# Attention over 64 row tiles: where V's bias, the output copy and one exponential stand in a tile, and x's normalisation as a three-operand pass

## The chip, the cores and the metric

The program runs on one core of a Trainium2 chip. The metric is the device time of one execution in microseconds (us); the kernel before takes 6042.36 us (median of 3 runs, 6042.21 to 6044.77). The engines are named as in the profile: PE (TensorE matmul), PEld (its weight load), DVE (VectorE), ACT (ScalarE), POOL (GpSimd), SP (SyncE, which issues the DMAs here).

## The reference, cut to what matters

Four layers run one after the other over x of shape (8, 1024, 256), each on a layer-normalised input and with a residual. Only the first is touched:

```
x = x + attn(layernorm(x))            # 16 heads of 16, per batch of 1024 rows
  q, k, v = x@Wq.T+bq, x@Wk.T+bk, x@Wv.T+bv
  logits  = li[:, :, None, :] + lj[:, None, :, :] + rel_b      # 3 relations for each pair (i, j)
  bias    = einsum('bijk,hk->bhij', softmax(logits), logical_bias)
  gate    = sigmoid(x @ gate_W.T + gate_b)                     # one for each row and head
  scores  = q.k/sqrt(16) + gate*bias
  out     = softmax(scores) @ v @ Wo.T + bo
x = x + fp8 layer;  x = x + mixer and MLP;  x = x + gated FFN  # unchanged
```

## The kernel before, in words

`attention` works through 64 tiles of 128 query rows, 8 tiles to a batch. A tile is a hand-written software pipeline: each engine has a `body` that loops `for u in range(H)` over the 16 heads, and the `if` lines in it say after which head the side work stands. Every engine runs its list strictly in that order; the engines meet at semaphores.

The main line for head h: PE makes the scores in `ps_s` (`pe_s`, L647); DVE adds the relation bias to the row (`dve_f`, L491, for 12 heads; POOL does it for heads 1, 4, 8 and 12 in two passes, L408 and L410); DVE adds the scores and takes the row minimum (`dve_s`, L502, a pass and a short read of the accumulator, called s(h) here); ACT takes the exponential (`act_e`, L576, e(h)); PE transposes the row (`pe_t`, L658, t(h)); ACT copies it to `AT` (`act_at`, L585, AT(h)); PE multiplies by V (`pe_pv`, L670). There is one `ps_s`, so PE's scores of head h+1 wait for s(h).

Side work, some for this tile, some for others:

- x's normalisation, one tile more than a batch ahead: `dve_ln` (u = 2), `pool_rstd`, then `dve_xn` (L440, u = 5), which frees the x buffer and lets PE transpose it (`pe_xT`, u = 6).
- V's bias: PE makes V and the gate's logits in `ps_m` at u = 3 (`pe_v`, L635); `dve_v` adds the biases (L455 to V, L459 to `zg`). `ps_m` is shared by many small products in a fixed order (`pm`, `pm_free`).
- The output of the tile before: ACT copies `ps_o` out (`act_o`, L589), PE transposes it (`pe_oT`, L680, u = 5; it also needs `dve_v` to have released `ps_m`), DVE normalises (`dve_norm`, L508 and L510, u = 6).
- The relation probabilities of the next tile: DVE L474 and L477, POOL L382 twice, ACT three exponentials, POOL sums them (L387, L391), ACT takes the logarithm and then the exponential of it, a reciprocal (`act_y0`, L568 and L571), POOL multiplies (L395), DVE corrects (`dve_y`, L482, u = 10), POOL multiplies twice (L400).

The first 56 tiles also prepare a tile of the next batch (`pro` is true); the last 8 don't, and have no `dve_xn` and no `dve_v`. `look` (there is a next tile) and `post` (there is one before) are true nearly always.

Of the kernel before, what the change touches and what calls it, by code (L numbers as in the profile page):

```python
# [13 lines left out]
P = 128  # L14
# [3 lines left out]
B, S, D = 8, 1024, 256  # L18
# [16 lines left out]
def wait(eng, sem, value):  # L35

    if isinstance(value, int) and value <= 0:
        return
    eng.wait_ge(sem, value)
# [10 lines left out]
def attention(nc, x_in, wqk, wvg, bqk, rows, ident_in, parts_d, x_out):  # L50
# [13 lines left out]
    with ExitStack() as ctx:  # L64
# [3 lines left out]
        def sem(name):  # L68
            HELD["done"].append(ctx.enter_context(nc.semaphore(name)))
            return HELD["done"][-1]  # L70
# [28 lines left out]
        xt = sb("xt", [P, 2, D])  # L99
        stats = sb("stats", [P, 6])  # L100
        mv = sb("mv", [P, 2])
        ve = sb("ve", [P, 1])
        mhalf = sb("mhalf", [P, 1])
        rstd = sb("rstd", [P, 1])
        xn = sb("xn", [P, D])
# [61 lines left out]
        x_free = sem("x_free")  # L167
# [269 lines left out]

        def dve_xn(dve, p, k):
            wait(dve, rstd_ok, p + 1)
            nc.vector.tensor_scalar(xn[:], xt[:, k, :], mv[:, 0:1], rstd[:, 0:1],  # L440
                                    ALU.subtract, ALU.mult).then_inc(x_free, 1)

        def dve_qk(dve, p):
            wait(dve, gT_ok, p + 1)
# [39 lines left out]
        def dve_f(dve, t, k, h):  # L484
            if h in POOL_HEADS:
                return
            r = rows_sb[h % NROW]
            if h == 0:
                wait(dve, pc_ok, t + 1)
            wait(dve, t_ok, 2 * (H * t + h) + 2)  # L490
            nc.vector.scalar_tensor_tensor(r[:], ps_p[:], rho[:, h:h + 1], R[k][0][:],  # L491
                                           ALU.mult, ALU.add).then_inc(fd_ok, 1)

        def dve_s(dve, t, k, slot, h):

            if h in POOL_HEADS:
                wait(dve, fp_ok, NPH * t + POOL_HEADS.index(h) + 1)
            else:
                wait(dve, fd_ok, NDH * t + DVE_HEADS.index(h) + 1)
            alone(dve, qk_ok, H * t + h + 1, dve_own)  # L500
            r = rows_sb[h % NROW]
            nc.vector.tensor_tensor_reduce(r[:], r[:], ps_s[:], small[:, slot, h:h + 1], BIG, ALU.add, ALU.min,  # L502
                                           nmax[:, h % NROW:h % NROW + 1]).then_inc(s_ok, 1)
# [50 lines left out]
        def act_rel(act, t, k, slot, step):  # L554
            if step == 0:
                wait(act, rel_step, 2 * t + 2)
                nc.scalar.activation(R[k][0][:], RT[:], ACT.Exp, scale=-1.0).then_inc(rel_exp, 1)
            else:
                wait(act, rel_d, 2 * t + step)
                dst = (R[k][1], R2)[step - 1]  # L560
                nc.scalar.activation(dst[:], dst[:], ACT.Exp,
                                     bias=small[:, slot, H + step - 1:H + step]).then_inc(rel_exp, 1)

        def act_y0(act, t, step):

            if step == 0:
                wait(act, rel_sum, 2 * t + 2)
                nc.scalar.activation(R2[:], RT[:], ACT.Ln).then_inc(rel_y0, 1)  # L568
            else:
                act.wait_ge(rel_y0, 2 * t + 1)  # L570
                nc.scalar.activation(R2[:], R2[:], ACT.Exp, scale=-1.0).then_inc(rel_y0, 1)  # L571

        def act_e(act, t, h):
            wait(act, s_ok, H * t + h + 1)
            r = rows_sb[h % NROW]
            nc.scalar.activation(r[:], r[:], ACT.Exp, scale=-1.0, bias=nmax[:, h % NROW:h % NROW + 1]  # L576
                                 ).then_inc(e_ok, 1)
# [9 lines left out]
        def act_o(act, o):  # L587
            wait(act, pv_ok, 2 + HG * (o + 1))
            nc.scalar.copy(O4[:], ps_o[:]).then_inc(o_ok, 1)  # L589
# [166 lines left out]
        def after(par, ib, n):  # L756

            return (par * NT + ib + n) % (2 * NT)

        def followed(t, pro):  # L760

            return t > 0 and t <= (B - 1) * NT if isinstance(t, int) else pro
# [137 lines left out]
        def _(dve):  # L900
# [51 lines left out]
            def body(dve, t, k, par, ib, pro, post, look, before):  # L952
                for u in range(H):
                    if u + 1 < H:
                        dve_f(dve, t, k, u + 1)
                    dve_s(dve, t, k, after(par, ib, 0), u)
                    if look and u < 2:
                        dve_rel(dve, t + 1, 1 - k, after(par, ib, 1), u)
                    if pro and u == 2:
                        dve_ln(dve, t + AHEAD, 1 - k)  # L960
                    if u == 3 and (not isinstance(t, int) or t >= 2):
                        dve_out(dve, t - 2)
                    if pro and u == 5:
                        dve_xn(dve, t + AHEAD, 1 - k)
                    if pro and u == 4:
                        dve_v(dve, t + NT, 1 - par, ib)
                    if post and u == 6:
                        dve_norm(dve, t - 1)
                    if look and u == 10:
                        dve_y(dve, t + 1)  # L970
                    if pro and u == 13:
                        dve_gate(dve, t + NT)
                    if pro and u == 14:
                        dve_qk(dve, t + AHEAD)
                    if look and u == 15:
                        dve_f(dve, t + 1, 1 - k, 0)
# [68 lines left out]
        @block.scalar  # L1045
        def _(act):
            def start(act):
                act.wait_ge(w_ready, 1)
                act_g_t(act, 0)
                act_xT(act, NT)  # L1050
                act_g_d(act, 0)
                act_g_e(act, 0)
                act_d(act, NT, NT)
                for s in range(2):
                    act_g_hi(act, 0, s)
                act_g_t(act, 1)
                for s in range(2):
                    act_g_mid(act, 0, s)
                act_g_ge(act, 0)
                act_g_d(act, 1)  # L1060
                act_g_e(act, 1)
                act_rel(act, 0, 0, 0, 0)
                act_rel(act, 0, 0, 0, 1)
                act_rel(act, 0, 0, 0, 2)
                for s in range(2):
                    act_g_hi(act, 1, s)
                for s in range(2):
                    act_g_mid(act, 1, s)
                for step in range(2):
                    act_y0(act, 0, step)  # L1070
                act_p(act, 0, 0)
                act_hi(act, NT)
                act_g_ge(act, 1)
                act_mid(act, NT)
                act.wait_ge(g_st, 16 * 8)

            def body(act, t, k, par, ib, pro, post, look, before):
                for u in range(H):
                    act_e(act, t, u)
                    if post and u == 5:  # L1080
                        act_o(act, t - 1)
                    if pro and u == 7:
                        act_xT(act, t + AHEAD)
                    if look and u in (7, 8):
                        act_y0(act, t + 1, u - 7)
                    if u >= LAG:
                        act_at(act, t, u - LAG)
                    elif post:
                        act_at(act, t - 1, H + u - LAG)
                    if u == 0 and (not isinstance(t, int) or t >= 2):  # L1090
                        act_aT(act, t - 2)
                    if followed(t, pro) and u == 0:
                        act_hi(act, t - 1 + AHEAD)
                    if followed(t, pro) and u == 2:
                        act_mid(act, t - 1 + AHEAD)
                    if look and u in (1, 3, 4):
                        act_rel(act, t + 1, 1 - k, after(par, ib, 1), (1, 3, 4).index(u))
                    if pro and u == 6:
                        act_gate(act, t + NT, 1 - par, ib)
                    if pro and u == 10:  # L1100
                        act_d(act, t + AHEAD, after(par, ib, AHEAD))
                    if look and u == 13:
                        act_p(act, t + 1, 1 - k)

            def finish(act):
                for u in range(H - LAG, H):
                    act_at(act, TILES - 1, u)
                act_aT(act, TILES - 2)
                act_o(act, TILES - 1)
                act_aT(act, TILES - 1)  # L1110

            act.preload_act_table_set("natural_log_exp_and_others")
            act.sem_inc(at_ok, 2)
            run(act, start, body, finish)
# [1298 lines left out]
```

## Time and profile before

| | us |
|---|---|
| median of 3 runs | 6042.36 (6042.21 to 6044.77) |
| the profiled execution | 6042.3 |
| its span | 6040.5 |
| attention in it | about 2870: `dve_norm` of the last tile stands at 2866.8 |
| one tile of the first 56, in step | 43.27 |
| one tile of the last 8 | 42.08 |

The page shows the profile of one execution. Inside attention the four compute engines are all busy over three quarters of the time, so the page's shares don't name the one that bounds it; the order of events in one tile does. After the first few tiles the tiles repeat to within some hundredths of a us, but for two or three, so one tile can be read for all.

### The profile page before, as it was taken

What the parts mean: (1) busy time and instruction counts of PE and PEld (TensorE: products, weight loads), DVE (VectorE), ACT (ScalarE), POOL (GpSimd) and SP (SyncE); (2) the same over time, 40 slices, a digit from 0 to 9 for tenths busy, and PEclk for the clock granted to TensorE, in tenths of its full rate; (3) what the DMA queues carried; (4) which work ended last, traced back from release to release, by engine and by line L of the source; (5) the groups of instructions that cost most, each with busy time, mean ns of one, the idle gap of its engine ahead of it and who ended that gap; (6) DMA issues with size and microseconds to landing.
All of it is one profiled execution on the core that took longest, in us unless ns stands there. A gap on an engine that the chain in (4) does not pass through costs nothing. (4 is left out here: it accounts for less than half of the span.)

```text
span 6040.5 us, 114022 instructions
## 1 busy us (share of the span) xinstructions
PE 5365.8 (89%) x40162; PEld 3532.6 (58%) x40162; DVE 4701.5 (78%) x6099; ACT 4409.7 (73%) x7005; POOL 3704.9 (61%) x2010
## 2 busy tenths in 40 slices
PE   6888888898989898888799869999999979999999
PEld 4666666666666666655344345555555546666665
DVE  6999999999999999998888679999999942122221
ACT  4999999999999999999366678888888821111111
POOL 3888888888888888875100079999999930000000
PEclk8999999999999999999899889999999989999999
DMA  2121121212112121200355555555555521111110
GB/s 74 28 49 31 28 51 28 51 28 51 28 34 45 30 48 31 46 17 14 129 190 211 187 211 187 208 208 191 195 201 207 184 101 42 45 35 35 35 35 11
DMA packets 461255, 537.80 MB, mean 89 GB/s; under 512 B 237537, under 2 KB 337761, under 8 KB 460785
## 3 DMA queue, kind: packets, MB, share of 16 engines
q1 hardware_dynamic: 460784, 531.75, 28.0%
q8 instruction: 268, 4.39, 0.3%
q14 instruction: 203, 1.66, 0.1%
HBM read 370.31 MB, written 161.35 MB: 88 GB/s over the span
## 5 line engine op out<-in xcount | busy, mean ns | idle before, releaser
L502 DVE CUSTOM_DVE_ANT_0 srow<-srow,ps_s,small 128x1024 f32<-128x1024 f32 x1024 | 1304.0, 1273 | 63.5 <-issue 34.6
L576 ACT ACTIVATE srow<-srow,nmax 128x1024 f32<-128x1024 f32 x1024 | 1200.0, 1172 | 87.3 <-DVE nmax L502 78.3
L585 ACT COPY AT<-ps_t 128x512 f32<-128x512 f32 x2048 | 1110.5, 604 | 19.8 <-PE ps_t L658 18.8
L658 PEld LDWEIGHTS ps_t<-ident,srow 128*128 128x128 f32 x8192 | 954.9, 141 | 224.2 <-issue 36.3
L658 PE MATMUL ps_t<-ident,srow 128*128 128x128 f32 x8192 | 1068.7, 273 | 2.8 <-ACT AT L585 2.4
L1977 POOL TENSOR_TENSOR c_hc<-c_hs,c_cs 128x1024 f32<-128x1024 f32 x432 | 1009.9, 2364 | 61.2 <-DVE c_hs L2079 59.1
L491 DVE SCALAR_TENSOR_TENSOR srow<-ps_p,rho,R 128x1024 f32<-128x1024 f32 x768 | 975.3, 1270 | 0.0
L1938 PE MATMUL c_ps_y<-c_hc,c_ident 128*128 128x512 f32 x2048 | 944.8, 594 | 29.9 <-DVE c_y L2062 21.4
L2079 DVE TENSOR_TENSOR_SCAN c_hs<-c_da,c_pd 128x1024 f32<-128x1024 f32 x384 | 860.1, 2273 | 54.6 <-PE c_pd L1929 54.6
L647 PE MATMUL ps_s<-K,Q 96*128 96x512 bf16 x2048 | 617.1, 383 | 291.2 <-DVE nmax L502 265.3
L2022 ACT ACTIVATE c_sT<-c_dxT,c_bT 128x256 f32<-128x256 f32 x1536 | 668.4, 494 | 107.0 <-PE c_pd L1929 96.9
L410 POOL TENSOR_TENSOR srow<-srow,R 128x1024 f32<-128x1024 f32 x256 | 608.1, 2375 | 46.9 <-POOL srow L408 46.9
L670 PE MATMUL ps_o<-AT,V 128*32 128x128 f32 x16384 | 607.4, 278 | 0.0
L2215 POOL TENSOR_TENSOR d_rstd<-d_ve,d_mhalf 128x4 f32<-128x4 f32 x16 | 16.3, 1017 | 899.1 <-DVE d_ve L1222 899.1
L1938 PEld LDWEIGHTS c_ps_y<-c_hc,c_ident 128*128 128x128 f32 x2048 | 359.5, 190 | 344.9 <-issue 314.0
L1929 PEld LDWEIGHTS c_pd<-c_ident,c_sT 128*128 128x128 f32 x3072 | 353.9, 142 | 340.0 <-issue 198.1
L1929 PE MATMUL c_pd<-c_ident,c_sT 128*128 128x128 f32 x3072 | 407.4, 276 | 106.8 <-DVE c_hc L2086 79.6
L670 PEld LDWEIGHTS ps_o<-AT,V 128*32 128x32 f32 x16384 | 401.3, 109 | 129.3 <-issue 128.5
L2013 ACT ACTIVATE c_da<-c_dt,c_a_neg 128x1024 f32<-128x1024 f32 x384 | 435.8, 1135 | 1.7 <-issue 1.7
L647 PEld LDWEIGHTS ps_s<-K,Q 96*128 96x128 bf16 x2048 | 144.4, 97 | 476.0 <-DVE nmax L502 342.9
L1970 POOL TENSOR_TENSOR c_db<-c_dx,c_bs 128x1024 f32<-128x1024 f32 x128 | 302.1, 2361 | 121.4 <-DMA c_bs<-bc_d 121.4
L2242 DVE TENSOR_TENSOR d_x<-d_ps_y,d_y 128x512 f32<-128x512 f32 x32 | 22.1, 691 | 438.6 <-PE d_ps_y L2317 438.6
(256 smaller groups left out, 8576.5 us busy)
## 6 DMA issues: line engine op xcount, KB each, us to landing
c_cs<-bc_d SPq DMA_DIRECT2D x256, 512.0 KB, 4.3
c_bs<-bc_d SPq DMA_DIRECT2D x64, 512.0 KB, 6.5
Q<-parts_d SPq DMA_DIRECT2D x384, 64.0 KB, 2.3
parts_d<-parts SPq DMA_DIRECT2D x57, 384.0 KB, 3.4
K<-parts_d SPq DMA_DIRECT2D x168, 128.0 KB, 4.4
sz_d<-b_sz SPq DMA_DIRECT2D x16, 1024.0 KB, 7.1
xv_d<-b_xv SPq DMA_DIRECT2D x16, 1024.0 KB, 7.8
dt_d<-b_ab SPq DMA_DIRECT2D x16, 1024.0 KB, 4.2
```

Of the source, the lines that this page charges most:

```text
L491: nc.vector.scalar_tensor_tensor(r[:], ps_p[:], rho[:, h:h + 1], R[k][0][:], ALU.mult, ALU.add).then_inc(fd_ok, 1)
L502: nc.vector.tensor_tensor_reduce(r[:], r[:], ps_s[:], small[:, slot, h:h + 1], BIG, ALU.add, ALU.min, nmax[:, h % NROW:h % NROW + 1]).then ...
L576: nc.scalar.activation(r[:], r[:], ACT.Exp, scale=-1.0, bias=nmax[:, h % NROW:h % NROW + 1]).then_inc(e_ok, 1)
L585: nc.scalar.copy(AT[h % NAT][:, HG * half:HG * half + HG, :], ps_t[:, half]).then_inc(at_ok, 1)
L647: last = nc.tensor.matmul(ps_s[:, n * 512:(n + 1) * 512], Q6[k][:, h, :], K6[:, h, n * 512:(n + 1) * 512], start=True, stop=True)
L658: last = nc.tensor.transpose(ps_t[:, half, i, :], rows_sb[h % NROW][:, j * P:(j + 1) * P], ident[:])
L670: last = nc.tensor.matmul(ps_o[32 * i:32 * i + 32, j, :], V[par][:, n, h, :], AT[h % NAT][:, n, :], start=(n == 0), stop=(n == NT - 1))
L1929: last = nc.tensor.transpose(pd[:, c, k * P:(k + 1) * P], src[:, k, c * P:(c + 1) * P], ident[:])
L1938: last = nc.tensor.matmul(ps_y[:, c, cut], ident[:], hc[place((n, c)) % NHC][:, cut], start=n == 0, stop=n == NS - 1)
L1977: nc.gpsimd.tensor_tensor(hc[place((n, c)) % NHC][:], hs[place((n, c)) % NHS][:], cs[n % NCS][:], ALU.mult).then_inc(hp_ok, 1)
L2022: last = nc.scalar.activation(sT[i % NSC][:, k, :], dxT[p][:, k, :], ACT.Copy, scale=bT[p][:, k, n:n + 1])
L2079: nc.vector.tensor_tensor_scan(h, gain, push, 0.0, ALU.mult, ALU.add).then_inc(h_ok, 1)
```

## The change

Four edits, all in `attention`:

1. `dve_xn` is written as `scalar_tensor_tensor` (a pass with a column and a second tensor) in place of `tensor_scalar` (a pass with two columns). The second tensor is `rstd`, one column repeated over 256 elements.
2. `dve_v` stands at u = 5, behind `dve_xn`, in place of u = 4.
3. `act_o` stands at the end of u = 4, in front of e(5), in place of behind it.
4. The second step of `act_y0` (the exponential, L571) stands in front of e(8) in place of behind it.

```
 def dve_xn(dve, p, k):
     wait(dve, rstd_ok, p + 1)
-    nc.vector.tensor_scalar(xn[:], xt[:, k, :], mv[:, 0:1], rstd[:, 0:1],
-                            ALU.subtract, ALU.mult).then_inc(x_free, 1)
+    nc.vector.scalar_tensor_tensor(xn[:], xt[:, k, :], mv[:, 0:1], rstd[:, 0:1].broadcast_to([P, D]),
+                                   ALU.subtract, ALU.mult).then_inc(x_free, 1)
...
         if pro and u == 5:
             dve_xn(dve, t + AHEAD, 1 - k)
-        if pro and u == 4:
+        if pro and u == 5:
             dve_v(dve, t + NT, 1 - par, ib)
...
     for u in range(H):
+        if look and u == 8:
+            act_y0(act, t + 1, 1)
         act_e(act, t, u)
-        if post and u == 5:
-            act_o(act, t - 1)
...
-        if look and u in (7, 8):
-            act_y0(act, t + 1, u - 7)
+        if look and u == 7:
+            act_y0(act, t + 1, 0)
...
+        if post and u == 4:
+            act_o(act, t - 1)
```

On DVE, between s(4) (the first pair of L502 rows) and s(6) (the last), before; the names in L455 and L459 are V and the gate's logits:

```order
L502 ISA srow,nmax<-srow,ps_s,small 128x1024
L502 ISA nmax 128x1
L455 TENSOR_TENSOR V<-ps_m,row 128x16x16
L459 TENSOR_TENSOR zg<-ps_m,b_misc 128x18
L491 SCALAR_TENSOR_TENSOR srow<-ps_p,rho,R_0 128x1024
L502 ISA srow,nmax<-srow,ps_s,small 128x1024
L502 ISA nmax 128x1
L440 TENSOR_SCALAR xn<-xt,mv,rstd 128x256
L491 SCALAR_TENSOR_TENSOR srow<-ps_p,rho,R_0 128x1024
```

And the same place now:

```order
L502 ISA srow,nmax<-srow,ps_s,small 128x1024
L502 ISA nmax 128x1
L491 SCALAR_TENSOR_TENSOR srow<-ps_p,rho,R_0 128x1024
L502 ISA srow,nmax<-srow,ps_s,small 128x1024
L502 ISA nmax 128x1
L440 SCALAR_TENSOR_TENSOR xn<-xt,mv,rstd 128x256
L455 TENSOR_TENSOR V<-ps_m,row 128x16x16
L459 TENSOR_TENSOR zg<-ps_m,b_misc 128x18
L491 SCALAR_TENSOR_TENSOR srow<-ps_p,rho,R_0 128x1024
```

V's two additions are moved past one bias pass, s(5) and x's pass, and x's pass is another instruction.

On ACT, from the relation's last exponential (L561) at u = 4 to AT(6), before:

```order
L561 ACTIVATE R<-R,small 128x1024
L576 ACTIVATE srow<-srow,nmax 128x1024
L589 COPY O<-ps_o 128x512
L585 COPY AT<-ps_t 128x512 x2
L576 ACTIVATE srow<-srow,nmax 128x1024
...
L568 ACTIVATE R<-RT 128x1024
L585 COPY AT<-ps_t 128x512 x2
L576 ACTIVATE srow<-srow,nmax 128x1024
L571 ACTIVATE R<-R 128x1024
L585 COPY AT<-ps_t 128x512 x2
```

And now:

```order
L561 ACTIVATE R<-R,small 128x1024
L589 COPY O<-ps_o 128x512
L576 ACTIVATE srow<-srow,nmax 128x1024
L585 COPY AT<-ps_t 128x512 x2
L576 ACTIVATE srow<-srow,nmax 128x1024
...
L568 ACTIVATE R<-RT 128x1024
L585 COPY AT<-ps_t 128x512 x2
L571 ACTIVATE R<-R 128x1024
L576 ACTIVATE srow<-srow,nmax 128x1024
L585 COPY AT<-ps_t 128x512 x2
```

L589 has changed places with e(5), and L571 with e(8). No instruction is added or removed on any engine, and PE's, POOL's and SP's lists have the same order as before.

## Rows read from the trace of the kernel before

**Rows 1.** The page, busy time, share of the span and instructions of each engine.
```profile
PE 5365.8 (89%) x40162; PEld 3532.6 (58%) x40162; DVE 4701.5 (78%) x6099; ACT 4409.7 (73%) x7005; POOL 3704.9 (61%) x2010
```
**Rows 2.** Windows of two tiles: us, busy and (count) by engine, granted clock, DMA.
```profile
1009.90:1053.17 43.27, 38.65 (x466) 29.13 (x464) 41.06 (x61) 41.98 (x66) 36.49 (x23) 1.00 0.11 26
2652.48:2694.56 42.08, 34.13 (x426) 24.15 (x426) 38.35 (x51) 40.03 (x57) 31.11 (x17) 1.00 0.05 14
```
**Rows 3.** DVE's waits, 186 to 2529 us: us in total, times, longest.
```profile
DVE R L482 <- POOL RT L395: 25.9, 53, 0.5
DVE V L455 <- PE ps_m L635: 22.4, 54, 0.9
```
**Rows 4.** Timeline of DVE in one tile: start us, us, instruction, [idle before <-releaser].
```profile
1021.59 1.27 DVE L502 CUSTOM_DVE_ANT_0 srow<-srow,ps_s,small 128x1024 f32<-128x1024 f32 x1
1022.79 0.08 DVE L502 DVE_READ_ACCUMULATOR2_ANT nmax<- 128x1 f32 x1
1023.28 0.42 DVE L455 TENSOR_TENSOR V<-ps_m,row 128x256 f32<-128x256 f32 x1 [0.40 <-PE ps_m L635]
1023.62 0.17 DVE L459 TENSOR_TENSOR zg<-ps_m,b_misc 128x18 f32<-128x18 f32 x1
1023.70 1.27 DVE L491 SCALAR_TENSOR_TENSOR srow<-ps_p,rho,R 128x1024 f32<-128x1024 f32 x1
...
1026.09 0.64 DVE L440 TENSOR_SCALAR xn<-xt,mv,rstd 128x256 f32<-128x256 f32 x1
1026.65 1.27 DVE L491 SCALAR_TENSOR_TENSOR srow<-ps_p,rho,R 128x1024 f32<-128x1024 f32 x1
```
**Rows 5.** Timeline of POOL in the same stretch.
```profile
1024.20 2.38 POOL L410 TENSOR_TENSOR srow<-srow,R 128x1024 f32<-128x1024 f32 x1 [0.18 <-POOL srow L408]
1026.53 2.43 POOL L387 TENSOR_TENSOR RT<-R,R 128x1024 f32<-128x1024 f32 x1
```
**Rows 6.** Line L440: duration in ns, minimum/median/maximum.
```profile
L440 DVE TENSOR_SCALAR xn<-xt,mv,rstd x57: 404/642/2604, 20.6 to 2497.6; 128x256 f32<-128x256 f32 x57
```
**Rows 7.** Timeline, an irregular tile at 804 us.
```profile
804.59 2.60 DVE L440 TENSOR_SCALAR xn<-xt,mv,rstd 128x256 f32<-128x256 f32 x1
804.67 2.37 POOL L387 TENSOR_TENSOR RT<-R,R 128x1024 f32<-128x1024 f32 x1
```
**Rows 8.** Line L477, ns as in rows 6.
```profile
L477 DVE SCALAR_TENSOR_TENSOR RT<-Dj,small,RT x64: 1271/1274/2292, 56.2 to 2782.3; 128x1024 f32<-128x1024 f32 x64
```
**Rows 9.** Timeline of POOL and DVE at 94 us.
```profile
93.42 2.35 POOL L410 TENSOR_TENSOR srow<-srow,R 128x1024 f32<-128x1024 f32 x1 [0.18 <-POOL srow L408]
...
94.56 2.29 DVE L477 SCALAR_TENSOR_TENSOR RT<-Dj,small,RT 128x1024 f32<-128x1024 f32 x1
```
**Rows 10.** Timeline around the correction L482 in the regular tile, all engines.
```profile
1036.98 2.38 POOL L395 TENSOR_TENSOR RT<-RT,R 128x1024 f32<-128x1024 f32 x1 [1.01 <-ACT R L571]
...
1039.22 0.60 PE L647 MATMUL ps_s<-K,Q 96*128 96x512 bf16 x2
...
1039.40 1.23 DVE L482 SCALAR_TENSOR_TENSOR R<-RT,R 128x1024 f32<-128x1024 f32 x1 [0.50 <-POOL RT L395]
...
1040.54 1.27 DVE L502 CUSTOM_DVE_ANT_0 srow<-srow,ps_s,small 128x1024 f32<-128x1024 f32 x1
```
**Rows 11.** Timeline of ACT and PE in the same tile, parts.
```profile
1027.75 0.62 ACT L589 COPY O<-ps_o 128x512 f32<-128x512 f32 x1
...
1029.17 1.23 ACT L576 ACTIVATE srow<-srow,nmax 128x1024 f32<-128x1024 f32 x1
...
1035.73 1.08 ACT L571 ACTIVATE R<-R 128x1024 f32<-128x1024 f32 x1
...
1037.39 0.86 PEld L658 LDWEIGHTS ps_t<-ident,srow 128*128 128x128 f32 x8 [0.46 <-issue]
```
**Rows 12.** Timeline of DVE in one of the last tiles.
```profile
2670.45 0.26 DVE L508 RECIPROCAL rinv<-ps_m 128x16 f32<-128x16 f32 x1 [1.13 <-PE ps_m L680]
...
2680.21 1.23 DVE L482 SCALAR_TENSOR_TENSOR R<-RT,R 128x1024 f32<-128x1024 f32 x1 [0.67 <-POOL RT L395]
```

## The prediction

> **What bounds the kernel now.** I read the page's busy times first. PE's 5365.8 us are the most [rows 1], but only attention is changed, so I went to windows of one tile there. In step a tile takes 43.27 us, of which DVE is busy 41.06, ACT 41.98, PE 38.65 and POOL 36.49 [rows 2]. DVE idles 2.2 us a tile and ACT 1.3: each is almost full, and each waits for the other. DVE carries the closed line (s(h), PE's next scores, s(h+1)), so its list is to be followed in time, with ACT as a second limit close behind. DVE's waits name two places which the change touches: V's bias waits 0.4 us for PE (22.4 us in 54 times) and the correction L482 waits 0.5 us for POOL's L395 (25.9 us in 53 times) [rows 3].
>
> Then the timeline of one tile. V's addition L455 stands idle 0.40 us; s(5) follows, and x's pass starts at 1026.09 and takes 0.64 us [rows 4]. Alone that pass takes 0.40 [rows 6]. POOL's L410 runs from 1024.20 to 1026.58 [rows 5], and x's pass ends 0.15 us after it, at 1026.73. So x's pass is held while POOL's pass runs, for 0.49 us, and then streams. That is the key to the case: the moment at which DVE gets past x's pass is set by POOL, not by what DVE did before it. Where DVE came only 0.12 us before the end of POOL's pass, POOL's next pass L387 got in first and x's pass took 2.60 us [rows 7].
>
> **V behind x's pass.** Without V's two additions between s(4) and the next bias pass, that pass starts at 1022.79, when s(4) is done [rows 4]. A bias pass and an s take 2.39 us together (1023.70 to 1026.09), so DVE reaches x's pass at 1025.18, 0.91 earlier than before. V's wait of 0.40 is gone: PE has long finished V. But L410 still ends at 1026.58, since POOL's list is unchanged and hangs on things of u = 0 and 1.
>
> **x's pass as three operands.** Does it still wait for POOL? It has two inputs in SBUF, x and the repeated column. The nearest instruction is L477, with a column and two SBUF tensors too. It takes 1.27 us alone [rows 8]. Beside L410, which ended at 95.77, it took 2.29 and ended 1.08 behind POOL's pass [rows 9]. So this form is held like the other. I take it that a repeated column counts as a tensor: no row shows one beside POOL. L477's 1.08 us are for 1024 elements; for 256 I take 0.27. Then x's pass ends at 1026.85. A following instruction starts 0.08 before the end of its forerunner (1026.73 against 1026.65), L459 starts 0.34 behind L455, and the bias pass 0.08 behind L459 [rows 4]. So V starts at 1026.77, and the bias pass at 1027.19 against 1026.65: 0.54 us later. Of this 0.42 is V, which ran in the shadow of the POOL wait and now runs behind it, and 0.12 the slower form. Bounds: if the new form streams as fast as the old one (0.15), 0.42 later; if it pays a whole 256-element pass behind POOL (0.42, as L455), 0.69 later; if it isn't held at all, it starts at 1025.18, takes 0.42, and the bias pass starts at 1025.94, 0.71 earlier.
>
> The Trainium skill ("SBUF — State Buffer", section "Who interferes with whom") says that a DVE instruction with two SBUF inputs contends with a GpSimd instruction that reads SBUF, and that the one that starts second is blocked until the first is done. It makes no exception for a repeated column. By that rule the sum stays at 0.54 later and the unheld case drops out; L477 agrees, for full tensors. It speaks against this edit, and against x standing in front of V.
>
> **The exponential L571 in front of e(8).** L571 starts at 1035.73, and L395 starts at 1036.98, 0.17 behind its end; POOL had been idle for 1.01 [rows 10, 11]. One exponential earlier, about 1.1 us, and with everything behind s(6) 0.54 late, L571 ends at about 1036.25 and L395 at about 1038.8. DVE is ready for L482 at 38.90 before and 39.44 now. The wait of 0.50 goes completely. AT(6) stands behind both L571 and e(8) in either order, so ACT's later work does not move by this; e(8) comes 1.1 us later, and PE wants it only behind the scores s(11) needs, at 1039.2 or more. The scores for s(11) end at 1039.82 [rows 10] and, late by 0.54, at 1040.36; L482 at 39.44 lets s(11) start 1.14 later, at 1040.58. So they just do not take the place of the wait. Bounds of the refund: 0 to 0.50, and I take 0.50. Net for a tile: 0.54 - 0.50 = +0.04 us.
>
> **The output copy in front of e(5).** In the first 56 tiles it gains nothing: PE starts s(7)'s scores when s(6) is done, not when the copy is. e(5) comes 0.6 us later, and ACT does the same work up to AT(3). In the last 8 tiles there is neither x's pass nor V, and L508 waits 1.13 us for PE's transposes of that copy, L482 a further 0.67 [rows 12]. With the copy one exponential earlier, s(7) is next bound by PE's scores, some 0.9 us earlier (estimate: the 1.13 less what the round trip from s(6) leaves), and L571's move lets L482 follow. I take 1.0 us for each of 7 tiles, out of bounds of 0 to 1.8; ACT has 2.05 idle in such a tile [rows 2], so it can follow.
>
> **Sum.** 56 x (+0.04) = +2; 7 x (-1.0) = -7; together -5 us. The profiled execution has 6042.3 us (span 6040.5 and 1.8 around it), and the median of the runs is 6042.36, the same. 6042.3 - 5 = 6037.
>
> **Rivals.**
>
> A, the forecast: 6037. For it: x's pass ended 0.15 behind L410 in the regular tile, and rows 9. Its own range is 6028 to 6055: -0.1 to +0.25 us a tile, and 0 to -8 for the last tiles.
>
> B, x's pass escapes POOL (the repeated column does not queue): DVE is 0.71 earlier at s(6). ACT can't follow: e(6) starts at 1029.17 with no idle time ahead of it, and PE's t(7) already waits for AT(6) (0.46 idle) [rows 11]. So s(11)'s scores stay where they are, and what is won is L482's wait: 0.50. 56 x 0.50 = 28, and 7 for the last tiles: 6007. Against it: rows 9.
>
> C, slower: the lateness behind x's pass is not refunded. Place: e(6) now starts 0.54 late, all ACT work behind it too, through AT(6), t(7), the projections and the scores for s(11). These have only 0.2 us to spare, and ACT has 1.3 us of idle in a tile from which to recover. It decides if ACT or PE slips by more than that: then s(11) and the next tile start as late as s(6) did. 56 x 0.54 = 30, less 6: 6066. For it: ACT's 41.98 of 43.27.
>
> D, x's pass loses to L387 in every tile, as in rows 7: 1.96 us more, 56 times 110: 6152. It needs DVE to come within about 0.2 us of L410's end, and it comes 1.4 before; against it too that waits of 0.49 were won.
>
> **How the numbers follow.** A 0.60, B 0.18, C 0.15, D 0.04, the rest for what I don't see. The time is A's. What this measurement can tell from no change is 0.2%, 12 us. Faster by more: B, and 0.07 of A: 0.25. Slower by more: C, D and 0.04 of A, and a little of the rest: 0.24. Within: 0.51. The range takes in B's time and C's: 6006 to 6066. A's own range stands above.
>
> **What would show it.** In the changed kernel's regular tile x's pass (L440) should take about 1.65 us (1.40 held, 0.27 streamed) and end 0.27 behind L410; a median near 0.42 is B, one above 2 is D. V's wait should be zero. L482's wait for POOL should be gone, and the tile last 43.2 to 43.5 us; a tile of 43.8 with L482 unwaited is C, and one of 42.8 is B. In the last tiles L508 should wait under 0.3 us and the tile take about 41.1. The forecast is wrong above all if the repeated column behaves unlike a tensor, or if POOL's L410 itself moves against s(5).

## The result, and the profile after

The changed kernel takes 6085.5 us (median of 4 runs, 6084.0 to 6092.4) against 6042.28 for the one before: ratio 1.0074, 95% interval 1.0061 to 1.0086. It is slower by 43 us; 6037 was forecast. The profiled execution has a span of 6082.2 us, 41.7 more than before.

The places that I had worked out came out as forecast. The first fence is DVE in a regular tile of the changed kernel (start us, us, instruction), the second POOL there; they answer to [rows 4, 5].

```profile
282.88 1.68 DVE L440 SCALAR_TENSOR_TENSOR xn<-xt,mv,rstd 128x256 f32<-128x256 f32 x1
284.49 0.41 DVE L455 TENSOR_TENSOR V<-ps_m,row 128x256 f32<-128x256 f32 x1
284.82 0.16 DVE L459 TENSOR_TENSOR zg<-ps_m,b_misc 128x18 f32<-128x18 f32 x1
284.90 1.27 DVE L491 SCALAR_TENSOR_TENSOR srow<-ps_p,rho,R 128x1024 f32<-128x1024 f32 x1
...
297.06 1.22 DVE L482 SCALAR_TENSOR_TENSOR R<-RT,R 128x1024 f32<-128x1024 f32 x1
```
```profile
281.89 2.39 POOL L410 TENSOR_TENSOR srow<-srow,R 128x1024 f32<-128x1024 f32 x1 [0.18 <-POOL srow L408]
284.24 2.54 POOL L387 TENSOR_TENSOR RT<-R,R 128x1024 f32<-128x1024 f32 x1
```

L410 ends at 284.28 and x's pass at 284.56: held 1.40, then 0.28 streaming. V has no idle time ahead of it, nor has L482. The tile, by L477 from 272.00 to 315.29, takes 43.29 us; 43.31 was forecast.

What was not forecast is that this is the minority of tiles. Windows of four tiles in a row, the columns as in [rows 2]; the last but two is TensorE's granted clock:

```profile
227.24:272.00 44.76, 39.94 (x464) 30.28 (x464) 41.85 (x61) 42.20 (x64) 36.65 (x22) 0.96 0.11 28
272.00:315.29 43.29, 38.53 (x464) 29.12 (x464) 41.90 (x63) 41.99 (x64) 36.63 (x22) 1.00 0.12 29
315.29:360.09 44.80, 39.96 (x464) 30.37 (x464) 41.86 (x63) 42.46 (x64) 36.67 (x22) 0.96 0.12 28
360.09:404.94 44.85, 40.01 (x464) 30.42 (x464) 41.85 (x61) 42.24 (x64) 36.63 (x22) 0.96 0.11 28
```

Three of the four take 44.8 us, with the clock at 0.96; the one of 43.29 has 1.00. From tile 3 to tile 57 it is 37 of 54. PE is busy 1.4 us longer in the slow ones for the same 464 matmuls, ACT 0.2 to 0.5, DVE and POOL no longer. Here is PE's timeline within a slow tile. Behind it come two windows of this tile, the second where the granted clock stood at 0.50, which is 1.2 of 2.4 GHz, and then the first window's counterpart in the tile of 43.29:

```profile
238.43 0.61 PE L647 MATMUL ps_s<-K,Q 96*128 96x512 bf16 x2
238.88 1.04 PE L658 MATMUL ps_t<-ident,srow 128*128 128x128 f32 x8
240.33 0.66 PE L680 MATMUL ps_m<-ident,O 128*128 128x128 f32 x4 [0.41 <-ACT O L589]
242.66 1.03 PE L647 MATMUL ps_s<-K,Q 96*128 96x512 bf16 x2 [1.68 <-DVE nmax L502]
243.49 1.92 PE L658 MATMUL ps_t<-ident,srow 128*128 128x128 f32 x8
```
```profile
239.00:242.53 3.53, 1.57 (x13) 1.09 (x11) 3.53 (x5) 3.29 (x5) 3.25 (x3) 1.00 0.11 37
242.53:245.95 3.42, 3.29 (x22) 2.45 (x26) 2.75 (x7) 2.25 (x4) 2.48 (x2) 0.50 0.03 7
283.75:287.28 3.53, 1.58 (x13) 1.10 (x11) 3.53 (x5) 3.30 (x5) 3.26 (x3) 1.00 0.14 37
```

PE had 1.57 us of work in the 3.53 us before the clock fell: it stood idle 0.41 us, waiting for ACT's output copy, and then 1.68 us, waiting for DVE's s(6). The tile of 43.29 has the same two pauses, and 1.58 us of work in the same stretch, and keeps its clock; so these pauses bring a fall in most tiles, not in all. At half clock PE's next eight transposes take 1.92 us in place of 1.04 and the scores 1.03 in place of 0.60. The clock recovers after 3.42 us and falls again in a later tile. The trace after has 37 tiles with such a fall between 150 and 2840 us, the trace before one.

DVE shows how that reaches the path. These are its passes s(7) and s(8) in the slow tile:

```profile
243.88 1.28 DVE L502 CUSTOM_DVE_ANT_0 srow<-srow,ps_s,small 128x1024 f32<-128x1024 f32 x1 [0.64 <-PE ps_s L647]
247.45 1.28 DVE L502 CUSTOM_DVE_ANT_0 srow<-srow,ps_s,small 128x1024 f32<-128x1024 f32 x1 [1.09 <-issue]
```

s(7) waits 0.64 us for its scores where it waits 0.21 in the tile of 43.29. s(8) waits 1.09, where it has no wait there: the profile names no releaser, but PE's scores for it end at 247.27, late behind the slow transposes. That is 0.43 + 1.09 = 1.52 us, which is what a slow tile is longer by the medians (44.81 against 43.29).

The sum over the spans. From tile 3 to tile 57 the changed kernel is 53.1 us longer, made up, to about 1 us, of 37 falls at 1.52 us each (44.81 against 43.29) and 0.02 us for each tile, less 5.4 us of two irregular tiles that only the trace before has. The last six intervals are 5.4 us shorter, 0.90 each (five take 41.20 in place of 42.10). The start is 2.7 us shorter. What follows the last L477 is 3.3 shorter, 0.9 of it still in attention and 2.4 in layers that the change doesn't touch: 53.1 - 5.4 - 2.7 - 3.3 = 41.7. The start and those layers vary by some us among all the kernels here (tile 3 begins between 183.8 and 188.5 us), so nothing is read from them.

### The profile page after: what moved, and what is told of

Same layout as the page of the kernel before. It is cut to its first block and busy times, and to the rows that moved or that the text cites. A ratio compares the mean times of both kernels' runs of the same rounds, so it can differ in the third digit from the quotient of the medians.

```text
span 6082.2 us, 114022 instructions
## 1 busy us (share of the span) xinstructions
PE 5411.7 (89%) x40162; PEld 3575.8 (59%) x40162; DVE 4744.7 (78%) x6099; ACT 4419.6 (73%) x7005; POOL 3714.1 (61%) x2010
## 3 DMA queue, kind: packets, MB, share of 16 engines
q14 instruction: 202, 1.65, 0.1%
## 5 line engine op out<-in xcount | busy, mean ns | idle before, releaser
L502 DVE CUSTOM_DVE_ANT_0 srow<-srow,ps_s,small 128x1024 f32<-128x1024 f32 x1024 | 1305.3, 1275 | 130.7 <-issue 89.3
L658 PEld LDWEIGHTS ps_t<-ident,srow 128*128 128x128 f32 x8192 | 984.1, 144 | 229.1 <-issue 29.0
L658 PE MATMUL ps_t<-ident,srow 128*128 128x128 f32 x8192 | 1098.6, 278 | 10.3 <-ACT AT L585 10.3
L410 POOL TENSOR_TENSOR srow<-srow,R 128x1024 f32<-128x1024 f32 x256 | 608.3, 2376 | 46.9 <-POOL srow L408 46.9
L670 PE MATMUL ps_o<-AT,V 128*32 128x128 f32 x16384 | 624.4, 283 | 0.0
L400 POOL TENSOR_TENSOR R<-R,R 128x1024 f32<-128x1024 f32 x126 | 297.2, 2381 | 123.4 <-DVE R L482 123.4
```

Source lines behind the costliest of these rows:

```text
L658: last = nc.tensor.transpose(ps_t[:, half, i, :], rows_sb[h % NROW][:, j * P:(j + 1) * P], ident[:])
L670: last = nc.tensor.matmul(ps_o[32 * i:32 * i + 32, j, :], V[par][:, n, h, :], AT[h % NAT][:, n, :], start=(n == 0), stop=(n == NT - 1))
```

## The experiments

Each is an edit of the changed kernel, or of the one before where said so. "Falls" counts how often the clock was at half between 150 and 2840 us in the profiled execution (one in a tile, but for one tile of e2_two_columns with two); the one or two falls of the kernels that have so few all stand in the first tiles, the last one or an irregular tile near 800 or 890 us. The tile is the median of those without a fall; the two idle times are PE's, in front of the output copy's transposes (L680) and in front of the scores for s(7). In the last two kernels a further 1.04 and 1.46 us stand in front of the scores for s(6), and 0.67 in the kernel before and in e1, e8 and e9.

| kernel | PE idle, us | tile, us | falls | median, us | ratio to before (95%) |
|---|---|---|---|---|---|
| before | 0.72, none | 43.27 | 1 | 6042.28 | |
| changed | 0.41, 1.68 | 43.29 | 37 | 6085.5 | 1.0074 (1.0061 to 1.0086) |
| e4_fill | 0.42, 0.81 | 43.30 | 0 | 6030.83 | 0.9983 (0.9974 to 0.9993) |
| e13_fill_once | 0.41, 1.25 | 43.30 | 7 | 6039.39 | 0.9997 (0.9987 to 1.0006) |
| e5_fill_elsewhere | 0.42, 1.70 | 43.29 | 37 | 6088.15 | 1.0079 (1.0062 to 1.0096) |
| e1_v_back | none, 1.16 | 42.88 | 1 | 6011.31 | 0.9953 (0.9936 to 0.9970) |
| e2_two_columns | 0.42, 1.55 | 43.15 | 43 | 6085.83 | 1.0074 (1.0057 to 1.0091) |
| e3_o_back | 1.45, 0.66 | 43.29 | 37 | 6091.9 | 1.0086 (1.0069 to 1.0103) |
| e7_v_alone | 1.45, 0.52 | 43.70 | 31 | 6089.59 | 1.0080 (1.0064 to 1.0097) |
| e8_y_alone | 0.72, none | 42.75 | 2 | 6008.93 | 0.9948 (0.9931 to 0.9965) |
| e9_three_alone | 0.71, 0.23 | 43.40 | 1 | 6045.6 | 1.0008 (0.9998 to 1.0018) |
| e6_v_first | 0.42, 1.14 | 42.75 | 2 | 6003.71 | 0.9940 (0.9923 to 0.9956) |
| e11_x_behind_v_4 | none, 0.48 | 42.70 | 1 | 6004.0 | 0.9939 (0.9922 to 0.9955) |
| e12_x_before_v_4 | none, 0.48 | 42.97 | 2 | 6013.86 | 0.9954 (0.9938 to 0.9971) |

**Does the clock cause the loss? e4_fill.**

```
 def pe_oT(pe, o, p_done):
-    for j in range(HG):
+    for j in list(range(HG)) * 3:
         last = nc.tensor.transpose(ps_m[:, j * P:(j + 1) * P], O4[:, j, :], ident[:])
```

> The changed kernel, in which PE makes the four transposes of the output copy (L680) three times over, with the same result, before it signals: 1.3 us more PE work inside the 1.68 us that PE now idles in front of the scores of s(7). Clock theory: the 44.8 us tiles exist because TensorE's granted clock falls to its lower level (0.5) behind that idle; with the idle cut to some 0.4 us the falls go, all tiles take 43.29, and 36 x 1.5 = 54 us come back: about 6030. Rival (lateness of ACT and PE not refunded, the clock a bystander): added PE work can't help, 6084 or more.

It took 6030.83 us, 55 less than the changed kernel, with more work and nothing else altered. PE's timeline in one tile:

```profile
457.33 1.04 PE L658 MATMUL ps_t<-ident,srow 128*128 128x128 f32 x8
458.79 1.53 PE L680 MATMUL ps_m<-ident,O 128*128 128x128 f32 x12 [0.42 <-ACT O L589]
461.13 0.60 PE L647 MATMUL ps_s<-K,Q 96*128 96x512 bf16 x2 [0.81 <-DVE nmax L502]
461.57 1.04 PE L658 MATMUL ps_t<-ident,srow 128*128 128x128 f32 x8
```

The filler added 0.87 us, not 1.3, and the regular tiles take 43.30 with no fall. This is also what the change costs and gives without the clock: 11 us faster than before, where the forecast was 5. Of the 10.8 us between the two spans, 5.3 lie in the last six intervals; the rest is mostly the irregular tiles of the trace before, the start and the layers behind, which the forecast did not count. The rival, that the lateness itself is what is lost, falls.

**As much work elsewhere: e5_fill_elsewhere.**

```
 def pe_wo(pe, o, p_done):
-    for c in range(DC):
+    for c in list(range(DC)) * 2:
         last = nc.tensor.matmul(ps_m[:, 0:D], attnT[:, c, :], w_o[:, c, :], ...
```

> The changed kernel with as much PE work added at another place: the output projection (L696) is made twice over at u = 1, with the same result, in front of an idle of 1.24 us at u = 2. If it is the idle around s(7) that lets the clock fall, 37 falls stay and the time stays near 6085. If PE's work in a tile as a whole counts, the falls go as with the transposes repeated: near 6030.

6088.15 us and 37 falls: no effect. PE's idle of 1.24 us at u = 2 shrank to 0.38, and that did not help either. One window over most of attention, of the kernel before, the changed one, e4_fill, e5_fill_elsewhere and e13_fill_once (one fence each):

```profile
190.00:2500.00 2310.00, 2059.43 (x24701) 1551.56 (x24702) 2189.05 (x3199) 2235.93 (x3407) 1944.02 (x1173) 1.00 0.17 37
```
```profile
190.00:2500.00 2310.00, 2058.61 (x24160) 1559.98 (x24160) 2180.84 (x3126) 2200.02 (x3334) 1908.53 (x1149) 0.97 0.17 37
```
```profile
190.00:2500.00 2310.00, 2101.34 (x25170) 1598.94 (x25168) 2233.10 (x3202) 2238.91 (x3412) 1955.03 (x1175) 1.00 0.17 38
```
```profile
190.00:2500.00 2310.00, 2103.18 (x24368) 1599.41 (x24367) 2180.60 (x3126) 2198.70 (x3334) 1908.49 (x1149) 0.97 0.17 37
```
```profile
190.00:2500.00 2310.00, 2078.67 (x24845) 1577.32 (x24844) 2222.57 (x3186) 2231.70 (x3397) 1945.22 (x1169) 0.99 0.17 37
```

e4_fill and e5_fill_elsewhere have PE busy for the same 2101 and 2103 us, but the clock at 1.00 and 0.97. And PE is no busier before than after (2059 against 2059). PE's mean share does not show the danger; the place of its idle time does.

**Half the filler: e13_fill_once.** The same edit as e4_fill with `* 2`.

> The changed kernel with PE's transposes of the output copy made twice, not three times: half of the filler. PE's idle between t(3) and s(7) sums to about 1.65 us, between the 1.56 of the kernel with V first (no falls of the clock) and the 1.96 of the one with x's pass in two columns (43 falls). Clock theory with a graded effect: fewer falls than 37, or none; 6030 without any, 6060 with half. If only the full filler helps: near 6085.

7 falls and 6039.39 us. The effect is graded: at an idle of 1.25 us behind one of 0.41 it happens in 7 of 54 tiles.

**Which edit makes the idle? e1_v_back and e2_two_columns, e3_o_back.** Each undoes one edit of the changed kernel.

```
# e1_v_back                                  # e2_two_columns
-if pro and u == 5:  dve_v(...)              -scalar_tensor_tensor(xn, xt, mv, rstd.broadcast, ...)
+if pro and u == 4:  dve_v(...)              +tensor_scalar(xn, xt, mv, rstd, ...)
# e3_o_back
-if post and u == 4: act_o(act, t - 1)       (at the end of u = 4)
+if post and u == 5: act_o(act, t - 1)       (behind e(5))
```

> The changed kernel with V's bias at its old place, u = 4; the other three edits stay. Clock theory: V runs before POOL's pass ends, so s(6) is 0.42 us earlier and the idle of PE in front of s(7) shrinks from 1.68 to about 1.2 us; the kernel before had an idle of 1.24 at another place with the clock at full, so no falls: a tile of about 42.9 (0.12 late at x's pass, 0.50 refunded at L482), 56 x (-0.4) - 6 = -28, about 6014. Rival (the new place of V costs nothing, the other edits carry the loss): still about 6084.

> The changed kernel with x's pass as before (two columns). Clock theory: x's pass is still held by L410, ends 0.13 us earlier, PE's idle is 1.55 in place of 1.68; tiles without a fall take 43.2, and falls stay or become fewer: 6035 to 6084. Rival (the three-operand form is what makes it slow): back to 6042 or below.

> The changed kernel with the output copy behind e(5) as before. Clock theory: PE's transposes of the copy move about 1 us later, to the middle of PE's idle, and split it into some 1.4 and 0.7 us; if the length of one idle counts, the falls go: about 6040 (tiles of 43.29, the last tiles 0.3 to 0.9 us longer than now). If the sum of idle in that stretch counts, falls stay: about 6088. Rival (the copy's place has no part in it): 6084 and 37 falls as before.

With V back at u = 4 the kernel takes 6011.31 us: the loss turns into a gain of 31. So V's new place is what loses, 74 us between the two kernels, of which the tiles give 56 x 0.41 = 23 by V's own time behind x's pass (42.88 against 43.29), and 36 x 1.52 = 55 by the clock.

x's pass in two columns brings nothing back: 6085.83. It ends 0.13 us sooner (1.55 in place of 1.68), which a tile without a fall shows (43.15 against 43.29), and it has 43 falls in place of 37: six more at 1.5 us each cost about what 0.14 us in each tile gives. The ends that I had given, 6035 to 6084, were just missed.

The output copy behind e(5) splits the idle into 1.45 and 0.66, and the falls stay at 37. Of the two readings that I had set against each other, the longest single idle and the idle in that stretch taken together, the first falls. In the last tiles it costs 0.14 us (41.34 against 41.20). The other 6 us by which its span exceeds that of the changed kernel lie in the start (3.1) and behind the last L477 (2.6), and no run here explains them.

**V's move alone: e7_v_alone.** The kernel before, with

```
-                    if pro and u == 4:
+                    if pro and u == 5:
                         dve_v(dve, t + NT, 1 - par, ib)
```

> The kernel before with V's bias alone moved to u = 5 behind x's pass. The sum of held x and V is 0.42 us later in each tile, and L482's wait is not there to refund it, as ACT is late too: 43.69 for a tile without a fall, 56 x 0.42 = 24, 6066. With the falls of the clock in two thirds to three quarters of the tiles, which the clock theory expects from an idle as long as in the changed kernel, 1.5 us each: 6120 to 6130.

The tile without a fall is 43.70 us, 0.43 more than before, as worked out. The time, 6089.59, is well under my 6120 to 6130: there are 31 falls, where I had counted on some 40, and each costs 1.13 us (44.83 against 43.70), not 1.5, since L482's wait is still in this kernel and takes up part of it. In DVE's waits it comes 23 times, nearly all in tiles without a fall, where the kernel before had 53 [rows 3]:

```profile
DVE R L482 <- POOL RT L395: 11.7, 23, 0.7
```

**L571's move alone: e8_y_alone.** The kernel before, with edit 4 only.

```
+                    if look and u == 8:
+                        act_y0(act, t + 1, 1)
                     act_e(act, t, u)
...
-                    if look and u in (7, 8):
-                        act_y0(act, t + 1, u - 7)
+                    if look and u == 7:
+                        act_y0(act, t + 1, 0)
```

> The kernel before with the exponential L571 alone moved in front of e(8). L482's wait of 0.50 goes: a tile of 42.77, in the last tiles 0.67 at most; 28 + 4: about 6010, no falls. If ACT bounds the tile instead (e(8) later), no change: 6042.

6008.93 us, and a tile of 42.75: the 0.50 of L482's wait comes back in full. It is the edit that carries the gain, 32 us (6040.78 for the kernel before in the runs made beside it). In the last tiles it gives 0.76 of the 0.90 (41.34 against 42.10).

**The three-operand form alone: e9_three_alone.** The kernel before, with edit 1 only.

> The kernel before with x's pass alone in three operands. The pass is held as before and ends 0.12 to 0.14 us later behind POOL's, and nothing refunds it: a tile of 43.40, 56 x 0.13 = 7, 6049; no falls. If the form or its hold on the port cost more (POOL's next pass is kept waiting), above 6060.

Its tile is 43.40, 0.13 longer than 43.27, as x's pass is (median 0.77 in place of 0.64). The whole time can't tell it from none: 1.0008, 0.9998 to 1.0018.

**Better orders: e6_v_first, e11_x_behind_v_4, e12_x_before_v_4.** All keep the two ACT moves and x's pass in two columns.

```
# e6_v_first:        u == 5: dve_v, then dve_xn
# e11_x_behind_v_4:  u == 4: dve_v, then dve_xn
# e12_x_before_v_4:  u == 4: dve_xn, then dve_v
```

> V's bias at u = 5 but in front of x's pass, x's pass with two columns as before, both ACT moves kept. V then runs inside the time in which x's pass would be held: the bias pass behind is as early as before the change, the wait of L482 goes: a tile of 42.77. PE's idle in front of s(7) should be about 1.1 to 1.2 us behind one of 0.4. Clock theory with these at full clock: 56 x (-0.50) - 6 = -34, 6008. If this sum of 1.5 us of idle is enough for falls: above 6060.

> A trial of a better order: x's pass in two columns directly behind V's bias at u = 4 (both ACT moves kept). DVE comes to it 0.3 us before POOL's L408 ends, so it should be held 0.3 and then get in ahead of L410: about 0.46 at u = 4 in place of a pass held 0.5 at u = 5. A tile of 42.5 to 42.8, 5990 to 6006. If it loses to L410 it is held 2.4 us: 6110 or more.

> The same with x's pass in front of V's bias at u = 4, inside V's wait of 0.40 for PE. DVE comes to it 0.13 us before POOL's L376 ends. If it gets in ahead of L408, x's pass costs nothing and a tile takes about 42.2, near ACT's 42.0 of work: 5975. If L408 gets in first, as L387 did at 804 us in the kernel before with 0.12 us to go, it is held until L408 ends, 1.2 us: a tile of 43.3 to 43.5, near 6040.

e6_v_first takes 6003.71 us and e11_x_behind_v_4 6004.0, both 0.6% faster than the kernel before, and the best here; they can't be told apart. In the first, V fills the time in which x's pass would stand held; in the second, x's pass (0.46 us) slips in between two POOL passes. DVE and POOL in e6_v_first, then in e11_x_behind_v_4:

```profile
453.33 2.38 POOL L410 TENSOR_TENSOR srow<-srow,R 128x1024 f32<-128x1024 f32 x1 [0.18 <-POOL srow L408]
454.31 0.42 DVE L455 TENSOR_TENSOR V<-ps_m,row 128x256 f32<-128x256 f32 x1
454.73 1.14 DVE L440 TENSOR_SCALAR xn<-xt,mv,rstd 128x256 f32<-128x256 f32 x1
455.67 2.42 POOL L387 TENSOR_TENSOR RT<-R,R 128x1024 f32<-128x1024 f32 x1
```
```profile
448.60 1.12 POOL L408 TENSOR_SCALAR srow<-R,rho 128x1024 f32<-128x1024 f32 x1
448.98 0.42 DVE L455 TENSOR_TENSOR V<-ps_m,row 128x256 f32<-128x256 f32 x1 [0.40 <-PE ps_m L635]
449.41 0.46 DVE L440 TENSOR_SCALAR xn<-xt,mv,rstd 128x256 f32<-128x256 f32 x1
449.90 2.38 POOL L410 TENSOR_TENSOR srow<-srow,R 128x1024 f32<-128x1024 f32 x1 [0.18 <-POOL srow L408]
```

e12_x_before_v_4 comes to x's pass 0.13 us before POOL's L376 ends. In most tiles L408 gets in first and x's pass is held a second time; in some it wins:

```profile
452.34 1.38 DVE L440 TENSOR_SCALAR xn<-xt,mv,rstd 128x256 f32<-128x256 f32 x1
452.45 1.11 POOL L408 TENSOR_SCALAR srow<-R,rho 128x1024 f32<-128x1024 f32 x1
...
624.24 0.41 DVE L440 TENSOR_SCALAR xn<-xt,mv,rstd 128x256 f32<-128x256 f32 x1
624.36 1.30 POOL L408 TENSOR_SCALAR srow<-R,rho 128x1024 f32<-128x1024 f32 x1
```

Its tiles take 42.97 and 42.70, and 42.70 is also what e11_x_behind_v_4 has. I had expected 42.2 for a pass that costs nothing. Something else then sets the tile at 42.70, and no run looked for it.

This kernel also bears on the falls. PE in one of its tiles, then in a slow tile of e7_v_alone:

```profile
456.57 0.60 PE L647 MATMUL ps_s<-K,Q 96*128 96x512 bf16 x2 [1.46 <-DVE nmax L502]
457.01 1.04 PE L658 MATMUL ps_t<-ident,srow 128*128 128x128 f32 x8
457.89 0.60 PE L680 MATMUL ps_m<-ident,O 128*128 128x128 f32 x4
458.97 0.60 PE L647 MATMUL ps_s<-K,Q 96*128 96x512 bf16 x2 [0.48 <-DVE nmax L502]
```
```profile
287.79 0.66 PE L680 MATMUL ps_m<-ident,O 128*128 128x128 f32 x4 [1.45 <-ACT O L589]
288.98 1.03 PE L647 MATMUL ps_s<-K,Q 96*128 96x512 bf16 x2 [0.53 <-DVE nmax L502]
```

The two pauses sum to 1.94 us in the first and 1.98 in the second, but 1.92 us of work lie between them in the first and 0.66 in the second. The first has no fall in a regular tile, the second 31. e1_v_back is like the first: 0.67 and 1.16 with as much work between, and no fall in a regular tile. So the sum of the pauses does not decide alone; what the falls go with is pauses close to each other.

## Why the prediction was wrong

The mechanism on DVE, POOL and ACT was right, and its sizes too. x's pass was forecast at 1.65 us and took 1.68; the next bias pass 2.01 us behind its start, and it was 2.02; L482's wait gone; 43.31 for a tile, and it is 43.29; 41.1 for a last tile, and it is 41.2. The repeated column is held like a full tensor, so rival B falls. That the pass is held says little by itself, since the two-column form is held as well (1.40 us in e2_two_columns); but it then streams in 0.28 us, a quarter of L477's 1.08 for four times the elements, where two columns take 0.15. The Trainium skill's rule ("SBUF — State Buffer", "Who interferes with whom") holds here for a repeated column too. Rival D did not happen: with 1.40 us to go x's pass always got in ahead of L387. Rival C, the lateness not refunded, is not it either, though it has the right sign: the tile without a fall is at 43.29, so the refund was whole.

The step that failed is in the part on V behind x's pass. I priced "0.54 us later" for the engine that is late, DVE, and for what it sets off in ACT and POOL, and counted PE's waiting for s(6) as free, since PE is not the engine that bounds the tile. No term of the sum stood for it. It is not free: the late s(6) brought PE's pauses together into one stretch with 2.1 us of idle, and behind it the granted clock fell to 0.50 in two tiles out of three. Each fall costs 1.52 us on the path, 55 us in all, where the rest of the sum was about -11 (e4_fill). What should have warned me was there: PE's granted clock of 1.00 in [rows 2], which a change of timing can lose, and one irregular tile of the kernel before that did lose it:

```profile
878.19:924.58 46.39, 40.16 (x464) 30.12 (x464) 42.66 (x63) 42.38 (x64) 35.69 (x23) 0.96 0.10 25
```

The clock fell there once, behind a pause of 2.00 us. No case of mine had it; the range ended at 6066.

The Trainium skill ("TensorE: Matmul & The Clock Gate", section "A second HAM failure mode: psum-queue depth-cycling") tells of a kernel whose TensorE pauses briefly between groups of matmuls, often enough for the clock to go back and forth between the two levels. The trace agrees: in the changed kernel no single pause shortly before a fall is longer than 1.71 us, and with 1.45 and 0.52 the clock fell as well (e7_v_alone).

In the last tiles the sum was right (0.90 for 1.0), but the shares were not: I gave most to the output copy, and the exponential alone gives 0.76.

What stays open: why two of three tiles fall and not all, though PE's pauses are the same in each, and what sets 42.70.

## What to carry to other kernels

Where an engine waits for a port or a unit that another one holds, work placed in front of that wait is free as long as it fits into it, and work placed behind it is paid in full. V's bias in front of x's pass gives a tile of 42.75 (e6_v_first), behind it 43.15 (e2_two_columns). So let the instruction that will be held come last. Before you count a longer wait of TensorE as free because it doesn't bound the kernel, read its granted clock in the stretch behind that wait. If it stands at its upper level with pauses close by, a few tenths of a us of further pause can cost more than all the terms that you summed: between the same two kernels PE's second pause goes from 1.14 to 1.55 us, and 42 of 54 tiles fall. To test it, repeat a matmul with the same result inside the pause: if more work makes the kernel faster and the falls are gone, it was the clock.

## What the runs showed of the hardware

A useless 0.87 us of PE work in each tile made a kernel 55 us faster (6085.5 to 6030.83); as much work about 12 us earlier in the tile (e5_fill_elsewhere) did nothing.

A DVE pass with one column and one repeated column waits for POOL's pass like one with two SBUF tensors, and streams its 256 elements in 0.28 us behind it; the two-column form needs 0.15. Which of the two engines went next went with how long DVE had stood waiting when POOL's pass ended: with 0.31 us or more DVE was first in each regular tile (e11_x_behind_v_4, and 0.49, 0.98 and 1.40 in others), with 0.12 to 0.14 POOL in 46 cases of 50 (e12_x_before_v_4). That the time waited is the cause is not shown.
